# Two sets of tiny TensorE products half a row group later in the second convolution

## The reference

```
feats   = 4 depthwise 7-tap convolutions of gn(x): horizontal, vertical, both diagonals
context = mean(feats * feats)                    # per image: 4 directions x 96 channels
hid     = leaky_relu(context @ w_att1.T, 0.2)    # 48 values per image
attn    = softmax((hid @ w_att2.T).reshape(4, 96), over the 4 directions)
x1      = x + conv3x3(sum_d attn[d] * feats[d], w_proj)

out     = x1 + L1(gn(x1))   # linear attention, FFT-based query, 3x3 depthwise on k/v, a projection
```

## Time and profile before

| what | value |
|---|---|
| median of 3 runs | 3841.41 us (3840.19 to 3842.67) |
| the profiled execution's own time | 3844.74 us |
| its span, first to last instruction | 3843.1 us |
| PE busy | 95% of the span, 22946 matmuls |
| DVE busy | 79% |
| ACT busy | 43% |
| mean clock granted to PE | 0.979 |

### The profile page before, as it was taken

How to read it: one execution, slowest core, us unless ns; L and a number is a source line. 1 busy time by engine, 2 the same in 40 slices (tenths; PEclk the granted TensorE clock), 3 DMA queues, 4 the chain that set the end, 5 groups by cost and what they waited for, 6 DMA issues and landing times.

```text
span 3843.1 us, 59619 instructions
## 1 busy us (share of the span) xinstructions
PE 3649.9 (95%) x22946; PEld 2998.9 (78%) x22946; DVE 3024.8 (79%) x2829; ACT 1642.1 (43%) x2720; POOL 211.1 (5%) x376
## 2 busy tenths in 40 slices
PE   4659999999999999999999999999999999999998
PEld 2348688968789688886889687896888878897977
DVE  7988998789877898779987898878987798854020
ACT  3422682138521584126821386215841268211630
POOL 1001000100001000010001000010000100010000
PEclk8779999999999999999999999999999999999999
DMA  5355222922147231742229222471317422271002
GB/s 116 98 137 132 66 67 35 225 73 69 48 102 182 59 83 42 167 121 67 66 37 226 71 68 51 110 182 48 87 41 173 112 67 66 39 178 32 1 7 31
DMA packets 164730, 344.35 MB, mean 90 GB/s; under 512 B 110336, under 2 KB 110576, under 8 KB 164432
## 3 DMA queue, kind: packets, MB, share of 16 engines
q1 hardware_dynamic: 141392, 255.36, 27.0%
q0 software_dynamic: 23040, 84.95, 10.0%
HBM read 189.27 MB, written 150.99 MB: 89 GB/s over the span
## 4 chain that ended last, share of the span: by engine, by line
PE 56%; DVE 22%; issue 19%; DMA 1%; ACT 1%; SPq 0%; DVEq 0%; POOL 0%; ACTq 0%; POOLq 0%
DVE feat L715 18%; PE banks L970 11%; PE banks L971 11%; PE banks L976 11%; PE banks L985 6%; PE banks L995 3%; PE banks L1053 3%; PE banks L1015 2%; PE banks L1001 2%; PE banks L1002 2%; PE banks L1039 1%; DMA feat<-feats_d 1%; DVE e_lo L747 1%; DVE e_hi L739 1%; PE banks L1008 0%
## 5 line engine op out<-in xcount | busy, mean ns | idle before, releaser
L715 DVE SCALAR_TENSOR_TENSOR feat<-xin,w,feat 96x1536 f32<-96x1536 f32 x540 | 947.1, 1809 | 1.8
L970 PE MATMUL banks<-e_hi,wp_hi 96*96 96x384 f32 x1728 | 587.4, 340 | 24.3 <-DVE e_lo L848 12.2
L970 PE MATMUL banks<-e_hi,a_hi 96*96 96x384 f32 x1728 | 597.7, 347 | 0.0
L971 PE MATMUL banks<-e_lo,a_hi 96*96 96x384 f32 x1728 | 592.9, 344 | 0.0
L971 PE MATMUL banks<-e_lo,wp_hi 96*96 96x384 f32 x1728 | 586.2, 340 | 0.0
L715 DVE SCALAR_TENSOR_TENSOR feat<-xin,wh,feat 96x1536 f32<-96x1536 f32 x288 | 520.7, 1808 | 28.9 <-ACT feat L497 27.2
L715 DVE SCALAR_TENSOR_TENSOR feat<-xin,wv,feat 96x1536 f32<-96x1536 f32 x288 | 520.8, 1808 | 0.0
L509 ACT ACTIVATE squares<-feat 96x1536 bf16<-96x1536 f32 x192 | 285.2, 1485 | 445.0 <-DVE feat L715 443.0
L976 PE MATMUL banks<-e_hi,a_lo 96*96 96x384 f32 (+1 forms) x1728 | 337.5, 339 | 0.0
L976 PE MATMUL banks<-e_hi,wp_lo 96*96 96x384 f32 (+1 forms) x1728 | 335.7, 338 | 0.0
L575 ACT ACTIVATE res<-banks 96x768 f32<-96x768 f32 x96 | 77.2, 804 | 598.7 <-PE banks L976 598.7
(11 more groups left out here) (152 smaller groups left out, 4854.1 us busy)
## 6 DMA issues: line engine op xcount, KB each, us to landing
feats_d<-feat SPq DMA_DIRECT2D x160, 576.0 KB, 4.1
feat<-feats_d SPq DMA_DIRECT2D x160, 576.0 KB, 6.8
feat<-in_x SPq DMA_DIRECT2D x48, 576.0 KB, 6.9
res<-in_x POOLq DMA_DIRECT2D x96, 288.0 KB, 4.1
out<-x POOLq DMA_DIRECT2D x96, 288.0 KB, 2.8
out<-res POOLq DMA_DIRECT2D x96, 288.0 KB, 4.3
xin<-in_x SPq DMA_DIRECT2D x32, 792.0 KB, 9.0
xin<-in_x SPq DMA_DIRECT2D x16, 684.0 KB, 10.2
```

The source lines that it names most:

```text
L715: dve.scalar_tensor_tensor(out=dst, in0=src, scalar=taps_w[d](k), in1=dst, op0=ALU.mult, op1=ALU.add).then_inc(tap_done, 1)
L970: pe.matmul(dst, whi[:, t, :], rows(e_hi, a0, n, dx), start=(t == CENTRE_FIRST[0]), stop=False)
L971: pe.matmul(dst, whi[:, t, :], rows(e_lo, a0, n, dx), start=False, stop=False)
```

## The change

In turns 1 to 7 PE issues `hidden` ahead of half (8, 0) of the second convolution in place of half (7, 1), and `logits` ahead of half (8, 1) in place of (8, 0). `HID_AT` is 7 in both. Nothing else is changed: the same instructions run, in the same order on every engine but PE, and turns 0 and 8 are as they were.

```
                 if second:
-                    attention_block(b - 1, {(HID_AT, 1): hidden, (HID_AT + 1, 0): logits} if first else {})
+                    attention_block(b - 1, {(HID_AT + 1, 0): hidden, (HID_AT + 1, 1): logits} if first else {})
                 elif first:
                     hidden()
                     logits()
```

## The result

The changed kernel takes 3811.8 us in the median (3809.8 to 3815.0, 4 runs), the kernel before 3841.8 in the same runs: a ratio of 0.9923, interval 0.9906 to 0.9940, 30 us less. A second set of runs gave 0.9931 (0.9918 to 0.9945), 3814.4 against 3840.4. I had forecast 3803, with 3794 to 3824 as the range: the direction is right, the time is in the range, and some 10 us of the likeliest case's gain are missing. The profiled execution took 3815.0 us (span 3813.4) against 3844.7.

The account below looks back on a forecast made before the run. PE was taken to set the pace, with DVE on the path at `hidden`. Wait 21.3 + clock 19 - new waits 2 = 38 us off the 3841.4 median gave 3803 us, range 3794 to 3824.

Parts of the forecast that it names:

- likeliest case: Whole kernel: wait and slow clock at `hidden` go, 2 us of new waits come; 38 us saved, 3803 us, chance 71%.
- The wait at `hidden`: PE at line 1115, turns 1 to 7: seven waits of 3.04 us for DVE's line 811 vanish, saving 21.3 us.
- The margin: At `hidden`: PE would arrive 1.8 us after DVE's line 811 ends and so not wait.
- `ready(8)`: Wait for the copy of group 6, newly ahead of `hidden`; ACT would finish it 1.5 us before PE comes.
- case E: At `hidden`: the wait only moves because PE still comes first; no change, 3841 us, chance 2%.
- The clock: 12 us windows from `hidden`, turns 1 to 7: without the wait PE's clock stays up, saving 19 us, bounds 12 and 33.
- The distance to the sums: From `logits` to the first convolution's later groups: 4.79 us less each turn, up to 12 us of PE waits, 2 charged.
- With those 2 us regained: DVE's first sum: its 2.01 us wait for `res` goes, so new PE waits cost 2 us for all seven turns.
- rival B: Group 4, first convolution: DVE regains nothing, PE waits 12 us; 3813 us, chance 12%; sign: line 970 waiting over 2 us.
- the 1.6 us of the earlier trace: Turn 7, ahead of `hidden`: DVE's line 811 was said to come 1.6 us behind ACT's last squares.
- No clock charged to waits of 1 to 2 us: New PE waits for sums: so near to idle stretches of about 1 us that no clock loss was charged.
- Rivals C and D: Clock falls at new waits: C, B plus clock loss, 3833 us, 5%; D, group 4 loses more than saved, 3855, 2%.

Follow-up runs that it names:

- mid_half: The kernel before with `hidden` moved between the high and low matmuls of half (7, 1), `logits` left at (8, 0): 3805.4 us, ratio 0.9911.
- fill_three: The kernel before with 3 extra matmuls of 480 columns ahead of `hidden` in turns 1 to 7, nothing moved: 3827.1 us, ratio 0.9965.
- after_again: The changed kernel run once more, unaltered, in a second set of runs: 3814.4 us, ratio 0.9931 to the kernel before.
- small_res: The changed kernel with `res` loads of groups 0 and 1 cut to 128 of 768 columns: 3805.5 us, ratio 0.9908 to the kernel before.
- logits_only: The kernel before with `logits` alone moved half a group later, to (8, 1), `hidden` staying at (7, 1): 3851.6 us, ratio 1.0028.
- one_more_half: The changed kernel with `hidden` at (8, 1) and `logits` at (9, 0), half a group later still: 3844.3 us, ratio 1.0009 to the kernel before.

## Why the prediction was right, and where it was off

*The wait at `hidden`*: 21.3 us predicted. mid_half and fill_three differ by it: 445.1 - 442.1 = 3.0 us a turn, 21. The margin was forecast as 1.8 us and is 1.73, and DVE's wait for `logits` as 5.4 and is 5.46. `ready(8)` held nothing up. Right; case E is out.

*The clock*: 19 us, with 12 and 33 as bounds. fill_three against the kernel before gives 447.4 - 445.1 = 2.3 us a turn, 16 in seven, and 13.7 by the medians. The mechanism was right, the term 3 to 5 us too large for the median run. The two profiled executions differ by 18.0 us (3844.7 - 3826.7), nearly the 19 that I read from one of them. So the profiled execution of the kernel before had probably lost more to the clock than the median run, and taking off another 3.3 us to get from it to the median counted that twice; no run tells the two apart.

*The distance to the sums*: the step that failed is "With those 2 us regained", and with it the term of 2 us. PE's new waits cost 443.6 - 442.1 = 1.5 us a turn, 9 in the six turns of that mean, and turn 7 had no such wait in this trace (the 7.7 us of the row are counted from the modelled end of the matmul ahead, so they leave a little out). The second trace, after_again, gives 0.9 a turn, and by the medians, each taken as the gain over the kernel before in its own set, it is 5.5 us (35.5 of mid_half less 30.0) and 8.9 us (34.8 of small_res less 25.9). So the price was 6 to 9 us and not 2.

The 2.01 us were those of turn 6: over turns 1 to 7 DVE had waited for `res` 15.8 us in 5 waits, the longest 5.9. DVE's wait at `res` did go, but not its lateness: 71.8 us from line 817 to the third sum before, 71.5 after. The load that freed it drew on the same DMA engines as the loads of its next chunk; DVE waited 4.20 us there. small_res shows that the `res` loads did this: without most of their bytes the waits are gone.

What happened is in the main rival B, to which I gave 12%: its time, 3813, is met (3811.8 and 3814.4), its price of 12 us was 6 to 9, and its place was group 3 as well as group 4. The sign that I had named for it, more than 2 us at group 4, did not come. The longest single wait was 0.94 us, and 1.41 in the second trace. In turn 6, where B asks for 1.9 us, it came as twice 0.94. In turn 1, where it asks for 3.0, it was 0.94, since the third sum came 1.5 us earlier behind line 817 than before. That the time is B's to 2 us is partly luck, since its clock term was too large by about as much as its price. The row with 97% DMA load should have weighed more than the 2.01 us of a wait. That the slack of the earlier trace rows is what counts was right, as logits_only and one_more_half show.

*A misreading*: the 1.6 us of the earlier trace rows are not the distance of line 811 from ACT's last squares. They are DVE's idle time between its last tap and the end of those squares, and lines 810 and 811 follow at once. So on the path ahead of `hidden` ACT's squares stand behind the taps. No term hung on it.

*No clock charged to waits of 1 to 2 us*: true of all waits in the first trace of the changed kernel, but not in general. In the second one the longest wait at a group, in turn 7, was 1.41 us, and the clock fell behind it:

```profile
3391.35 0.39 PE L970 MATMUL banks<-e_hi,wp_hi 96*96 96x384 f32 x1 [1.41 <-DVE x L800]
```
```profile
3390.00:3396.00 6.00, 4.65 (x19) 4.16 (x20) 5.77 (x7) 0.00 (x0) 1.03 (x2) 0.73 0.85 222
```

In all, from the turns: 21 + 16 - 9 = 28 us, against 30 in one set of runs and 26 in the other. Rivals C and D needed the clock to fall at each new wait; that is nearly what one_more_half did, at twice the distance.

## What to carry to other kernels

A wait of the bounding engine can cost more than its length: read the granted clock behind it before you price it. When a small step is moved later to spare one engine a wait, count the distance from it to every later meeting of the two engines, and find the smallest slack; here 3.2 us in place of 4.8 kept the gain and left out the price. Here a wait for a transfer that went away, with the DMA engines 97% busy in that stretch before the change, turned up at the next transfer, and work that needed no load, put ahead of work that did, covered it.

## What was not expected of the hardware

Waits of PE of 0.9 to 1.3 us were followed by the low clock in none of these traces and waits of 3 us each time (7 of 7 before). Between them it went either way: behind one of 1.41 us it fell, behind one of 1.89 it didn't. A fall took between 1.7 and 4.7 us of a 12 us window with the same wait ahead of it. The runs of logits_only lie 14 us apart (10 runs) and those of mid_half 3 (4 runs), but those of the kernel before, with the same waits of 3 us, only 5 (20 runs); what makes logits_only scatter isn't shown. And a 480-column fp32 matmul took 0.8 us of PE (the trace records it as two instructions) where one of 384 columns in the convolution's number format took 0.18.
